# Products of ones in two idle stretches of TensorE, and other places for single blocks' outputs, row numbers and rows

## The chip, the cores and the metric

One core of a Trainium2 chip runs the whole program as one launch. The metric is the device time of one execution in microseconds (us); the median of several executions counts.

## The reference, cut to what matters

Two layers work on x of 16 × 256 tokens with 128 features, all in float32:

```
xn = layernorm(x)
s  = attention_0(xn)           # 16 heads of 64, two null keys, l2-normed q and k, ALiBi, causal
g  = silu(experts_0(xn))       # top-1 of 8 experts: gelu(x W1[e] + b1[e]) W2[e] + b2[e]
x  = x + s * g
xn = layernorm(x)
s  = attention_1(xn)           # one head of 128, causal, then layernorm and Wfc
g  = silu(experts_1(xn))       # top-2 of 8 experts, the two outputs weighted by their gates
x  = x + s * g
```

W1[e] is 128 × 512 and W2[e] is 512 × 128.

## The kernel before

**Order of the stages.** The program begins with norms and projections (0 to 59 us in the profile), then does attention steps b = 0 to 5 of layer 0 (to 319 us). Next come the experts of layer 0 (319 to 407 us), steps 6 to 15 with the first parts of layer 1 woven in, attention of layer 1, the experts of layer 1 (877 to 1026 us), and the combination of the two expert outputs. Each engine has its instructions in an order written out by hand; they meet through counting semaphores.

**Before the first scores.** TensorE does `tokens(0)` (transposes, L1233), then a list `RING_FIRST` of jobs that share two PSUM banks in turn: twelve `unit`s (a 128×512 projection each, L1285), then `("qk", i, 0)` (four transposes of a normed q or k part, L1304) in turn with the units of batch 1. Ahead of the first `qk` stands `nulls()` (L1451 to L1456). A `qk` waits until GpSimd has scaled its part (L1086), which comes behind a chain of Newton steps on GpSimd (L1081), which comes behind sums of squares on VectorE (L1873). From the unit `("unit", 2, 1)` on, `tokens(g)` and `logits(g)` (L1241, matmuls with 8 moving columns) are put between; `tokens(g)` waits for four tiles of `second_norm` on VectorE (L407).

**The expert stages.** Tokens are sorted by expert into rows in DRAM. A stage works through blocks j = 0, 1, 2, ...: double blocks of 256 rows (15 in layer 0, 31 in layer 1) and then 9 single blocks of 128 rows (j = 15 to 23 and 31 to 39). Block j uses buffer q = j % 4 for its weights, input rows, outputs `yb[:, q]` and row numbers `idx[:, q]`. For a block the engines do this:

- SyncE, step j: wait for `ye_evac` of block j, load weights (L688, 514 KB) and bias (L689) of block j + 4; wait for `xT_evac` of block j + 2, load the rows of block j + 6 (L683). All are issues of one queue, each behind a value that is read from a table.
- TensorE, step j: `turn(j+2)` (transpose the rows, L764), `up(j+1)` (L772), `down(j)` (L783).
- ScalarE: `gelu(j+1)` (L818); in layer 0 also `half_tanh` (L828).
- VectorE, step j: in layer 0 `silu2(j-1)` (L877); then `evac_x(j+2)` (row numbers L859, turned rows L860), then `add_b2(j)` (L868 for a double, L866 for a single block).
- GpSimd: `send(j)`, an indirect DMA for each 128 rows of output (L738), which adds 16 to `sent{q}` when it has landed.

`evac_x(j)` overwrites the row numbers of buffer q, so it waits until all earlier sends from that buffer have landed:

```
v.wait_ge(S["xT_full"], j + (base + 1))
if layer or not isinstance(j, int) or j >= NBUF:
    v.wait_ge(S[f"sent{q}"], sends(layer, j, q, i))
```

With `evac_x(j+2)` ahead of `add_b2(j)` in VectorE's order, a late send of block j - 2 holds up both.

Of the kernel before, what the change touches and what calls it, by code (L numbers as in the profile page):

```python
# [17 lines left out]
NB, N, D = 16, 256, 128  # L18
# [21 lines left out]
PERIOD = ((4, 11), (4, 27))  # L40
assert all((u - NSMALL) % 2 == 0 for u in UNITS_OF) and (NBLK0, NBLK1) == (24, 40)
# [73 lines left out]
def block_kernel(nc, a):  # L115
# [9 lines left out]
    with ctx:  # L125
# [130 lines left out]
        warm = take(1)  # L256
        LAST = (0, 1, 3, 2, 4, 6, 5, 7)
# [22 lines left out]
        def part(n):  # L280
# [6 lines left out]
        TAB = (TAB0, [FX, UX, CGX, HALF, UNI, FIRST, STEPS, CMP, RSJ])  # L287
        th = RA[:, SIZES[5] + SIZES[6]:SIZES[5] + SIZES[6] + 4 * D].rearrange("p (i n) -> p i n", i=2)
# [377 lines left out]

        def sends(layer, j, q, i):

            before = layer * sum(16 if m in SMALL[0] else 32 for m in range(q, NBLK0, NBUF))
            if isinstance(j, int):  # L670
                return before + sum(16 if m in SMALL[layer] else 32 for m in range(q, j, NBUF))
            n = 16 if q in SMALL_OF_FOUR[layer] else 32
            return i * n + (before + 32 - n)

        def ffn_sync(sp, layer, nblk, base, scattered, first_rows=None):
# [8 lines left out]

            def load_weights(j, q, i):
# [45 lines left out]
        def ffn_send(pool, layer, nblk, base):  # L731
            yb, idx = FFNB[layer][5:7]
# [12 lines left out]
            quads(pool, first, last, send)  # L745
            for j in range(last + 1, nblk):
                send(j, j % NBUF, j // NBUF)

        def all_sent(eng, layer):

            for q in range(NBUF):
                eng.wait_ge(S[f"sent{q}"], sends(layer, (NBLK0, NBLK1)[layer], q, 0))
# [4 lines left out]
        def ffn_tensor(pe, layer, nblk, base, counts, between=None):  # L757
# [3 lines left out]
            def turn(j, q, i):  # L761
                pe.wait_ge(S[f"rows_in{q}"], (i + (counts[q] + 1)) * 16)
                for t in range(1 if single(layer, j, q) else 2):
                    mm = pe.transpose(XT[q % 2][:, t * P:(t + 1) * P], xb[:, q, t, 0:D], ident)  # L764
# [43 lines left out]
        def ffn_scalar(act, layer, nblk, base, counts):  # L808
            HB = HBANKS[layer]
            wb, hT, yb = FFNB[layer][0], FFNB[layer][3], FFNB[layer][5]  # L810
# [11 lines left out]
            def half_tanh(j, q, first=False):  # L822
# [5 lines left out]
                act.activation(th[:, q % 2, 0:n], yb[:, q, 0:n], ACT.Tanh, scale=0.5).then_inc(S["tanh_done"], 1)  # L828
# [21 lines left out]
        def ffn_vector(v, layer, nblk, base, counts, flat=2 * NBUF, behind=None, between=None):  # L850
            XT, YB = bank[0:2], bank[6:8]
            _, b2b, xb, _, xbT, yb, idx = FFNB[layer]

            def evac_x(j, q, i):
                v.wait_ge(S["xT_full"], j + (base + 1))
                if layer or not isinstance(j, int) or j >= NBUF:
                    v.wait_ge(S[f"sent{q}"], sends(layer, j, q, i))
                n = 1 if single(layer, j, q) else 2
                v.tensor_copy(idx[:, q, 0:n], xb[:, q, 0:n, D].bitcast(I32))  # L859
                v.tensor_copy(xbT[:, q % 2, 0:n * BLK], XT[q % 2][:, 0:n * BLK]).then_inc(S["xT_evac"], 1)  # L860

            def add_b2(j, q, i):
                v.wait_ge(S["ye_full"], j + (base + 1))
                v.wait_ge(S[f"w_in{q}"], (i + (counts[q] + 1)) * 32)
                if single(layer, j, q):
                    ins = v.tensor_tensor(yb[:, q, 0:D], YB[q % 2][:, 0:D], b2b[:, q], ALU.add)  # L866
                else:
                    ins = v.tensor_tensor(yb[:, q, :].rearrange("p (t d) -> p t d", t=2),  # L868
# [4 lines left out]
            def silu2(j, q):  # L873
# [3 lines left out]
                v.scalar_tensor_tensor(out=yb[:, q, 0:n], in0=th[:, q % 2, 0:n], scalar=1.0, in1=yb[:, q, 0:n], op0=ALU.add,  # L877
# [349 lines left out]
        def _(pe):  # L1227
# [46 lines left out]

            pe.wait_ge(S["const_in"], 16)
# [196 lines left out]
            for use in RING_FIRST:  # L1472
# [875 lines left out]
```

## Time and profile before

| what | us |
|---|---|
| median of 3 runs (1060.01, 1060.05, 1069.24) | 1060.05 |
| the profiled execution | 1055.93 |
| its span, first to last instruction | 1054.1 |
| its mean granted TensorE clock | 0.981 |

The span and every start time are of the one profiled execution; the 1.8 us around it are start and end of the program. In the page, TensorE's matmuls are busy for 92% of the span, VectorE for 66%, GpSimd for 62%, ScalarE for 60%.

### The profile page before, as it was taken

The page shows a single profiled execution, that of the slowest core. Times are in us where ns is not written, and L with a number is a line of the kernel's source. Part 1 is how long each engine was busy: PE and PEld are TensorE (multiplying, and loading weights), DVE is VectorE, ACT ScalarE, POOL GpSimd, SP SyncE. Part 2 cuts the span into 40 slices and gives each one's busy share as a digit, 9 for nine tenths or more (in the row PEclk, how much of TensorE's full clock was granted, in tenths as well). Part 3 has the DMA queues.
Part 4 walks back from the last instruction along what each step waited for, and adds up shares of the span by engine and source line. Part 5 has one row for each costly group of instructions (what it writes and reads, how often), then busy time and mean ns, then how long its engine had stood idle before and what let it go on. Part 6 is the DMA issues. An engine that isn't in the chain of part 4 may idle for free.

```text
span 1054.1 us, 21432 instructions
## 1 busy us (share of the span) xinstructions
PE 965.7 (92%) x6330; PEld 695.2 (66%) x6330; DVE 691.8 (66%) x2589; ACT 631.3 (60%) x1945; POOL 650.7 (62%) x803
## 2 busy tenths in 40 slices
PE   5788799999998978999999999999898899999965
PEld 2565466666668976666665665556666788999955
DVE  6977777886773324867778677677885574445634
ACT  4348767767765546677776775766665564444432
POOL 4663588788756543676686668788746651555540
PEclk9789999999999999999999999999999999999997
DMA  9400202302337764033031230321222035787758
GB/s 292 78 7 1 47 27 62 73 26 60 84 104 181 216 204 117 6 75 65 16 70 25 46 70 26 70 56 50 55 66 68 31 102 136 227 231 226 214 168 240
DMA packets 95444, 103.20 MB, mean 98 GB/s; under 512 B 10095, under 2 KB 83030, under 8 KB 95088
## 3 DMA queue, kind: packets, MB, share of 16 engines
q1 hardware_dynamic: 88752, 89.36, 33.4%
q0 software_dynamic: 6592, 12.65, 3.5%
q8 instruction: 45, 0.74, 0.3%
q14 instruction: 55, 0.45, 0.1%
HBM read 77.54 MB, written 23.50 MB: 96 GB/s over the span
## 4 chain that ended last, share of the span: by engine, by line
PE 54%; DVE 18%; ACT 8%; POOL 7%; issue 6%; DMA 5%; SPq 1%; POOLq 0%; DVEq 0%; ACTq 0%
PE bank L1285 10%; PE bank L772 7%; PE bank L1314 7%; PE bank L783 7%; PE bank L1341 5%; DVE arena L1973 5%; ACT arena L1697 4%; PE bank L1329 4%; PE bank L1304 4%; PE bank L1364 3%; DMA expert_out<-RA 2%; DVE arena L1982 2%; DMA expert_out<-arena 2%; POOL arena L1071 2%; DVE arena L1873 2%
## 5 line engine op out<-in xcount | busy, mean ns | idle before, releaser
L1697 ACT ACTIVATE arena<-arena 128x128 f32<-128x128 f32 (+1 forms) x512 | 226.9, 446 | 102.1 <-DVE arena L1973 101.8
L1973 DVE CUSTOM_DVE_ANT_0 arena<-bank,arena 128x128 f32<-128x128 f32 (+1 forms) x512 | 183.1, 413 | 115.2 <-PE bank L1314 112.3
L1285 PE MATMUL bank<-arena 128*128 128x512 f32 x384 | 211.4, 637 | 7.7 <-ACT arena L1686 5.2
L1071 POOL TENSOR_TENSOR arena<-arena 128x512 f32<-128x512 f32 x128 | 133.3, 1045 | 127.8 <-ACT arena L1673 108.7
L1982 DVE COPY arena<-bank 128x384 f32<-128x384 f32 x256 | 130.1, 549 | 21.3 <-PE bank L1329 21.0
L1086 POOL TENSOR_TENSOR arena<-arena 128x512 f32<-128x512 f32 x128 | 129.8, 1050 | 1.3
L1673 ACT ACTIVATE arena<-bank 128x512 f32<-128x512 f32 x192 | 112.7, 587 | 27.7 <-PE bank L1285 27.4
L1329 PEld LDWEIGHTS bank<-const,arena 128*128 128x128 f32 x768 | 91.4, 142 | 55.6 <-issue 55.2
L738 POOL DMA_INDIRECT expert_out<-arena x71 | 71.3, 1005 | 90.8 <-DVE arena L868 40.5
L1314 PE MATMUL bank<-arena 64*128 64x128 f32 (+1 forms) x1024 | 118.5, 350 | 6.6 <-DVE arena L1973 6.0
L1341 PE MATMUL bank<-arena 128*64 128x256 f32 (+1 forms) x1024 | 112.2, 340 | 6.6 <-DVE arena L1982 6.2
L818 ACT ACTIVATE arena<-bank,arena 128x256 f32<-128x256 f32 (+1 forms) x160 | 59.0, 451 | 85.1 <-PE bank L772 85.1
L1314 PEld LDWEIGHTS bank<-arena 64*128 64x128 f32 x1024 | 67.0, 186 | 65.0 <-issue 50.2
L1341 PEld LDWEIGHTS bank<-arena 128*64 128x64 f32 x1024 | 62.4, 136 | 68.9 <-issue 34.6
L638 POOL DMA_INDIRECT expert_rows<-XN,slots x92 | 91.8, 998 | 25.7 <-issue 19.4
L1329 PE MATMUL bank<-const,arena 128*128 128x128 f32 x768 | 106.1, 275 | 0.0
L1697 ACT ACTIVATION_READ_ACCUMULATOR arena<-arena 128x1 f32 x512 | 97.6, 191 | 0.0
L1873 DVE TENSOR_REDUCE arena<-arena 128x8 f32<-128x512 f32 x128 | 84.3, 679 | 13.4 <-POOL arena L1071 13.0
L1304 PE MATMUL bank<-const,arena 128*128 128x128 f32 x512 | 81.7, 289 | 11.0 <-POOL arena L1086 7.3
L1110 POOL TENSOR_TENSOR arena<-arena 128x512 f32<-128x512 f32 x64 | 79.6, 1276 | 14.8 <-DMA arena<-recip_rows 14.8
L1081 POOL TENSOR_TENSOR arena<-arena 128x64 f32<-128x64 f32 x192 | 60.8, 316 | 40.3 <-DVE arena L1886 26.1
L1285 PEld LDWEIGHTS bank<-arena 128*128 128x128 f32 x384 | 60.6, 194 | 33.5 <-issue 23.3
(302 smaller groups left out, 1641.3 us busy)
## 6 DMA issues: line engine op xcount, KB each, us to landing
arena<-in_wp SPq DMA_DIRECT2D x40, 514.0 KB
arena<-recip_rows SPq DMA_DIRECT2D x30, 512.0 KB, 6.4
XN<-in_wp SPq DMA_DIRECT2D x24, 514.0 KB
arena<-expert_rows SPq DMA_DIRECT2D x46, 129.0 KB
arena<-in_b SPq DMA_DIRECT2D x64, 64.0 KB
arena<-expert_out SPq DMA_DIRECT2D x16, 256.0 KB, 5.2
expert_out<-fill SPq DMA_DIRECT2D x11, 338.6 KB
expert_rows<-fill SPq DMA_DIRECT2D x1, 2644.5 KB, 21.7
```

Source lines behind the costliest of these rows:

```text
L1071: pool.tensor_tensor(sq[:, i % 2], r, r, ALU.mult).then_inc(S["sq_done"], 1)
L1086: pool.tensor_tensor(raw[:, t, 512 * k:512 * k + 512].rearrange("p (h d) -> p h d", d=DH), raw[:, t, 512 * k:512 * k + 512].rearrange("p ( ...
L1285: mm = pe.matmul(RING[bnk][:, :], xa[:, p, t * P:(t + 1) * P], wqkv[:, 512 * k:512 * k + 512], start=True, stop=True)
L1304: mm = pe.transpose(RING[bnk][:, P * c:P * c + P], raw[:, t, 512 * k + P * c:512 * k + P * c + P], ident)
L1314: mm = pe.matmul(SBANK[k][:, P * t:P * t + n], qT[r:r + 64, p, c, t * P:(t + 1) * P], kT[r:r + 64, p, c, 0:n], start=True, stop=True)
L1329: mm = pe.transpose(TBANK[k][:, P * j:P * j + P], SPb[:, c % 2, 384 * k + P * j:384 * k + P * j + P], ident)
L1341: mm = pe.matmul(OB[64 * k:64 * k + 64, N * (c % 2) + P * j:N * (c % 2) + N], Vt[:, p, j, DH * h:DH * h + DH], PTb[:, c % 2, 384 * k + N * ...
L1673: ins = act.activation(dst, src[:, :], ACT.Copy)
L1697: ins = act.activation(w, w, ACT.Exp, bias=nm[:, p, 16 * t + h:16 * t + h + 1], scale=-1.0, accum_out=den[:, p, 16 * t + h:16 * t + h + 1])
L1873: v.tensor_reduce(ss[:, t, 8 * k:8 * k + 8], sq[:, i % 2].rearrange("p (h d) -> p h d", d=DH), AX.X, ALU.add).then_inc(S["ss_done"], 1)
L1973: ins = v.tensor_tensor_reduce(out=SPb[:, c % 2, 384 * k + P * t:384 * k + P * t + n], in0=SBANK[k][:, P * t:P * t + n], in1=alibi[:, h, N ...
L1982: v.tensor_copy(PTb[:, c % 2, 384 * k:384 * k + 384], TBANK[k][:, 0:384]).then_inc(S["pt_evac"], 1)
```

## The change

**Products of ones.** TensorE multiplies the 128×128 tile `ones` with itself into a PSUM bank that nothing reads yet, 10 times at its start (behind `ones_ready`, ahead of the constants' wait and `tokens(0)`) and 20 times between `nulls()` and the first `qk`.

**Places.** A block's outputs and row numbers now have a place k = `PLACES[layer][j]`; places 0 to 3 are the old buffers, others are new memory (`OWN`). In layer 0 the single blocks j = 15 to 23 get places 4, 5, 6, 3, 0, 1, 2, 4, 5. The places from 4 on share one semaphore, `sent4`; `evac_x` waits on it once, at j = 22, for the sends of blocks 15, 16 and 17. `evac_x(18)` to `evac_x(21)` wait for the sends of blocks 11 to 14. In layer 1 each single block has a place of its own and `evac_x` waits for no send. Double blocks keep their buffers and waits.

**Rows of layer 1's single blocks.** They no longer go through the four row buffers. SyncE loads them into a tile `SROWS` with nine places: five of the loads stand in steps 1, 5, 9, 13 and 17, four in steps 20 to 23, each behind the step's weights. TensorE waits for all nine before it turns the first. The nine row loads of steps 25 to 33, with their waits, are gone.

```diff
+PLACES = (tuple(j % 4 if j < 15 else (4, 5, 6, 3, 0, 1, 2, 4, 5)[j - 15] for j in range(NBIG[0] + NSMALL)),
+          tuple(j % 4 if j < NBIG[1] else 4 + j - NBIG[1] for j in range(NBIG[1] + NSMALL)))
+AGAIN = (22, None)
@@ ffn_sync, step
                 load_weights(j + NBUF, q, i + 1)
-                if more:
+                if layer and q == 1 and not isinstance(j, int):
+                    load_single(i)
+                if layer and isinstance(j, int) and last <= j < last + NSMALL - last // NBUF:
+                    load_single(j - last + last // NBUF)
+                if more and not (layer and single(1, j + NBUF + 2 if isinstance(j, int) else j, q)):
                     sp.wait_ge(S["xT_evac"], j + (base + 3))
                     load_rows(j + NBUF + 2, (q + 2) % NBUF, i + (q + 2 + NBUF) // NBUF)
@@ ffn_send
-                        yt[layer][:, :], bass.IndirectOffsetOnAxis(ap=idx[:, q, t:t + 1], axis=0), yb[:, q, t * D:(t + 1) * D], None,
-                        bounds_check=(1 + layer) * T - 1, oob_is_err=False).then_inc(S[f"sent{q}"], 16)
+                        yt[layer][:, :], bass.IndirectOffsetOnAxis(ap=numbers(layer, j, q)[:, t:t + 1], axis=0),
+                        outputs(layer, j, q)[:, t * D:(t + 1) * D], None,
+                        bounds_check=(1 + layer) * T - 1, oob_is_err=False).then_inc(S[sender(layer, j, q)], 16)
@@ ffn_tensor, turn
+                if layer and single(1, j, q):
+                    pe.wait_ge(S["single_rows"], NSMALL * 16)
+                    mm = pe.transpose(XT[q % 2][:, 0:P], SROWS[:, j - NBIG[1], 0:D], ident)
@@ ffn_vector, evac_x
-                if layer or not isinstance(j, int) or j >= NBUF:
-                    v.wait_ge(S[f"sent{q}"], sends(layer, j, q, i))
+                if place(layer, j, q) < NBUF and (layer or not isinstance(j, int) or j >= NBUF):
+                    v.wait_ge(S[sender(layer, j, q)], sends(layer, j, q, i))
+                if j == AGAIN[layer]:
+                    v.wait_ge(S[f"sent{NBUF}"], sent_by(layer, NBUF, j))
@@ tensor
+            def keep_running(n, out):
+                for _ in range(n):
+                    pe.matmul(out[:, 0:P], ones[:, :], ones[:, :], start=True, stop=True)
+            pe.wait_ge(S["ones_ready"], 1)
+            keep_running(10, TBANK[1])
             pe.wait_ge(S["const_in"], 16)
             tokens(0)
...
                 if use == ("qk", 0, 0):
                     nulls()
+                    keep_running(20, TBANK[1])
```

## Rows read from the trace of the kernel before

**Rows 1.** The page, part 4: the chain that ended last, by engine.
```profile
PE 54%; DVE 18%; ACT 8%; POOL 7%; issue 6%; DMA 5%; SPq 1%; POOLq 0%; DVEq 0%; ACTq 0%
```

**Rows 2.** That chain in order of time: start, length, what.
```profile
9.40 4.54 DMA small<-in_L_attn_k_scale
...
33.98 1.05 POOL arena L1086
```

**Rows 3.** Timeline of TensorE, 0 to 75 us: start, length, work, [idle before].
```profile
9.21 1.09 PE L1233 MATMUL bank<-const,arena 128*128 128x128 f32 x4 [9.21 <-DVE arena L407]
...
35.17 2.09 PE L1304 MATMUL bank<-const,arena 128*128 128x128 f32 x8 [7.30 <-POOL arena L1086]
37.09 2.08 PE L1285 MATMUL bank<-arena 128*128 128x512 f32 x2
...
45.38 0.60 PE L1233 MATMUL bank<-const,arena 128*128 128x128 f32 x4
...
46.26 1.10 PE L1285 MATMUL bank<-arena 128*128 128x512 f32 x2
```

**Rows 4.** Busy by stretch: engines in order, then granted clock, DMA share, GB/s.
```profile
30.00:32.00 2.00, 0.00 (x0) 0.00 (x0) 1.86 (x21) 0.00 (x0) 1.63 (x5) 0.80 1.04 192
...
44.00:46.00 2.00, 2.00 (x9) 1.26 (x9) 2.00 (x6) 1.01 (x2) 1.04 (x1) 0.78 0.00 0
...
64.00:66.00 2.00, 1.77 (x12) 1.26 (x13) 0.81 (x7) 1.73 (x8) 1.61 (x6) 0.84 0.26 78
```

**Rows 5.** Timeline of VectorE, 42 to 52 us.
```profile
42.03 1.08 DVE L407 TENSOR_SCALAR arena<-RS_,small,arena 128x128 f32<-128x128 f32 x1
...
43.73 2.96 DVE L407 TENSOR_SCALAR arena<-RS_,small,arena 128x128 f32<-128x128 f32 x8
...
51.39 0.25 DVE L1936 TENSOR_SCALAR arena<-bank,small 128x32 f32<-128x32 f32 x1 [1.73 <-PE bank L1462]
```

**Rows 6.** Waits of layer 0's singles, 370 to 410 us: total, times, longest.
```profile
DVE RA L859 <- DMA expert_out<-RA: 16.5, 9, 4.5
```

**Rows 7.** The same for layer 1's singles, 985 to 1030 us.
```profile
DVE arena L859 <- DMA expert_out<-arena: 13.9, 10, 2.5
```

**Rows 8.** Timeline of TensorE, layer 0's single blocks: up(16), up(17), up(23).
```profile
380.19 1.16 PE L772 MATMUL bank<-RS_,XN 128*128 128x128 f32 x8 [1.94 <-DVE RS_ L860]
...
382.19 1.12 PE L772 MATMUL bank<-RS_,XN 128*128 128x128 f32 x8
...
402.66 1.16 PE L772 MATMUL bank<-RS_,XN 128*128 128x128 f32 x8 [1.27 <-DVE RS_ L860]
```

**Rows 9.** Timeline of VectorE: add_b2(15).
```profile
382.28 0.29 DVE L866 TENSOR_TENSOR RA<-bank,arena 128x128 f32<-128x128 f32 x1 [0.18 <-PE bank L783]
```

**Rows 10.** Timeline of SyncE's queue, layer 0: rows (L683) and weights (L688).
```profile
378.19 0.50 SPq L683 DMA_DIRECT2D arena<-expert_rows  x1
...
383.94 0.34 SPq L688 DMA_DIRECT2D XN<-in_wp  x1
...
389.06 0.34 SPq L688 DMA_DIRECT2D XN<-in_wp  x1
...
390.68 0.34 SPq L683 DMA_DIRECT2D arena<-expert_rows  x1
391.79 0.34 SPq L688 DMA_DIRECT2D XN<-in_wp  x1
```

**Rows 11.** Busy by stretch, behind the load issued at 383.94.
```profile
388.00:388.50 0.50, 0.33 (x3) 0.33 (x3) 0.32 (x2) 0.15 (x1) 0.00 (x0) 1.00 0.38 107
```

**Rows 12.** Timeline of SyncE's queue, layer 1: weights of block 34.
```profile
1001.21 0.34 SPq L688 DMA_DIRECT2D arena<-in_wp  x1
```

**Rows 13.** Timeline of TensorE, layer 1: up(39).
```profile
1021.24 1.16 PE L772 MATMUL bank<-arena 128*128 128x128 f32 x8 [1.02 <-DVE arena L860]
```

**Rows 14.** DMA queues, layer 1's singles (1001 to 1018 us): packets, MB, share.
```profile
q1 hardware_dynamic: 2369, 3.56, 77.3%
q0 software_dynamic: 256, 0.39, 6.2%
```

More of the change, by code:

```diff
@@ L256, in block_kernel @@
         warm = take(1)
+        SROWS = take(NSMALL * ROW).rearrange("p (k d) -> p k d", k=NSMALL)
+        YROWS1 = take(NOWN[1] * ROW).rearrange("p (k d) -> p k d", d=ROW)
         LAST = (0, 1, 3, 2, 4, 6, 5, 7)
@@ L665, in entry, with place, outputs, numbers @@
             return i * (NBUF - len(few)) + (len(few) + q - k)
+        def place(layer, j, q):
+            return PLACES[layer][j] if isinstance(j, int) else q
+        def outputs(layer, j, q):
+            k = place(layer, j, q)
+            n = 1 if single(layer, j, q) else 2
+            return OWN[layer][:, k - NBUF, 0:D] if k >= NBUF else FFNB[layer][5][:, k, 0:n * D]
+        def numbers(layer, j, q):
+            k = place(layer, j, q)
+            n = 1 if single(layer, j, q) else 2
+            return OWN[layer][:, k - NBUF, D:D + 1].bitcast(I32) if k >= NBUF else FFNB[layer][6][:, k, 0:n]
+        def sent_by(layer, k, last):
+            return sum(16 if m in SMALL[layer] else 32 for m in range(last) if min(PLACES[layer][m], NBUF) == k)
+        def sender(layer, j, q):
+            return f"sent{min(place(layer, j, q), NBUF)}"
         def sends(layer, j, q, i):
-            before = layer * sum(16 if m in SMALL[0] else 32 for m in range(q, NBLK0, NBUF))
+            k = place(layer, j, q)
+            before = layer * sent_by(0, k, NBLK0)
             if isinstance(j, int):
-                return before + sum(16 if m in SMALL[layer] else 32 for m in range(q, j, NBUF))
-            n = 16 if q in SMALL_OF_FOUR[layer] else 32
-            return i * n + (before + 32 - n)
+                return before + sent_by(layer, k, j)
+            return i * 32 + before
         def ffn_sync(sp, layer, nblk, base, scattered, first_rows=None):
@@ L749, in all_sent @@
         def all_sent(eng, layer):
-            for q in range(NBUF):
-                eng.wait_ge(S[f"sent{q}"], sends(layer, (NBLK0, NBLK1)[layer], q, 0))
+            for k in range(NPLACES):
+                eng.wait_ge(S[f"sent{k}"], layer * sent_by(0, k, NBLK0) + sent_by(layer, k, (NBLK0, NBLK1)[layer]))
         HBANKS = (bank[2:6], bank[4:6] + bank[2:4])
@@ L761, in turn @@
             def turn(j, q, i):
-                pe.wait_ge(S[f"rows_in{q}"], (i + (counts[q] + 1)) * 16)
-                for t in range(1 if single(layer, j, q) else 2):
-                    mm = pe.transpose(XT[q % 2][:, t * P:(t + 1) * P], xb[:, q, t, 0:D], ident)
+                if layer and single(1, j, q):
+                    pe.wait_ge(S["single_rows"], NSMALL * 16)
+                    mm = pe.transpose(XT[q % 2][:, 0:P], SROWS[:, j - NBIG[1], 0:D], ident)
+                else:
+                    pe.wait_ge(S[f"rows_in{q}"], (i + (counts[q] + 1)) * 16)
+                    for t in range(1 if single(layer, j, q) else 2):
+                        mm = pe.transpose(XT[q % 2][:, t * P:(t + 1) * P], xb[:, q, t, 0:D], ident)
                 mm.then_inc(S["xT_full"], 1)
@@ L809, in ffn_scalar @@
             HB = HBANKS[layer]
-            wb, hT, yb = FFNB[layer][0], FFNB[layer][3], FFNB[layer][5]
+            wb, hT = FFNB[layer][0], FFNB[layer][3]
             def gelu(j, q, i):
@@ L827, in half_tanh @@
                 n = D if single(layer, j, q) else 2 * D
[L828 removed]
+                act.activation(th[:, q % 2, 0:n], outputs(layer, j, q), ACT.Tanh, scale=0.5).then_inc(S["tanh_done"], 1)
             def both(j, q, i):
@@ L851, in ffn_vector @@
             XT, YB = bank[0:2], bank[6:8]
-            _, b2b, xb, _, xbT, yb, idx = FFNB[layer]
+            _, b2b, xb, _, xbT, _, _ = FFNB[layer]
             def evac_x(j, q, i):
                 v.wait_ge(S["xT_full"], j + (base + 1))
-                if layer or not isinstance(j, int) or j >= NBUF:
-                    v.wait_ge(S[f"sent{q}"], sends(layer, j, q, i))
+                if place(layer, j, q) < NBUF and (layer or not isinstance(j, int) or j >= NBUF):
+                    v.wait_ge(S[sender(layer, j, q)], sends(layer, j, q, i))
+                if j == AGAIN[layer]:
+                    v.wait_ge(S[f"sent{NBUF}"], sent_by(layer, NBUF, j))
                 n = 1 if single(layer, j, q) else 2
-                v.tensor_copy(idx[:, q, 0:n], xb[:, q, 0:n, D].bitcast(I32))
+                ids = SROWS[:, j - NBIG[1]:j - NBIG[1] + 1, D] if layer and n == 1 else xb[:, q, 0:n, D]
+                v.tensor_copy(numbers(layer, j, q), ids.bitcast(I32))
                 v.tensor_copy(xbT[:, q % 2, 0:n * BLK], XT[q % 2][:, 0:n * BLK]).then_inc(S["xT_evac"], 1)
```

19 lines of the change are left out of this document (13 added, 6 removed).

## Prediction

> **What bounds the kernel now.** I read the chain of work that ended last first, by engine and then in order of time. TensorE holds 54% of it and VectorE 18% [rows 1]; no single engine is the bound, so each edit has to be priced where it stands. In order of time the chain leaves TensorE alone up to 35 us: it goes from a small load that lands at 13.94 through sums on VectorE to the Newton steps on GpSimd and the first scaled part at 33.98 [rows 2]. From 35.17 it is TensorE, which had stood idle for 7.30 us [rows 3]. Its granted clock fell in that gap and was back only near 45 us [rows 4]: at 37.09 a unit (x2) takes 2.08 us, at 46.26 the same takes 1.10 us [rows 3].
>
> In the expert stages I read the waits and then the timelines. In both layers' single blocks VectorE's longest waits are at L859, for a send to land: nine of them, 16.5 us, in layer 0 [rows 6] and ten, 13.9 us, in layer 1 [rows 7]. TensorE passes them on: up(16) and up(23) come behind waits of 1.94 and 1.27 us, while up(17), which found its rows, came 2.00 us behind up(16) [rows 8]. From up(17) to up(23) are 20.47 us, 3.41 for each block against 2.00 without waits.
>
> **Ten products at the start.** A float32 product has two records (a unit is x2). Four records took 1.09 us at 9.21 against 0.60 at 45.38 [rows 3], so the clock there is the lower of 1.2 and 2.4 GHz, although no fall is recorded. Twenty records at 0.27 us are 5.4 us, inside the 9.21 us in which TensorE is idle. They delay nothing. If they raised the clock in time, the first units would be faster, but up to 33.98 the chain is a load, VectorE and GpSimd [rows 2]. Price 0; on either side I leave 0.3 us.
>
> **Twenty products before the first qk.** Forty records of 128 columns at full clock cost about 0.125 us each (eight in 1.16 less the tail, [rows 8]): 5.0 us, from 27.87 to 32.9. The first qk can't start before GpSimd's part at 35.1 [rows 2], so they delay nothing, and 2.3 us of idle time are left where there were 7.30. Before, the fall came between 30 and 32 (a mean of 0.80, [rows 4]), over 2 us behind the last work. I take it that the clock stays up.
>
> What is the gain? At full clock the sequence from the second qk on, which GpSimd releases at 36.1, is: qk 0.5, unit 0.9, logits 0.8, then (qk 0.45, unit 0.9) twice, up to 41 us, where it stood at 45.38. Then `tokens(1)` waits for VectorE: four tiles end at 42.03 + 1.08 = 43.11 [rows 5]. That is the new limit: 45.38 − 43.11 = 2.27 us earlier. `tokens(2)` needs four of the eight tiles from 43.73 at 0.37 each, 45.2 us; it stood some 2.0 us later. VectorE itself waited 1.73 us at 51.39 [rows 5] and hardly elsewhere before the first scores, so it can follow by little more than that. **I take 1.9 us.** From below, 0 (the clock falls all the same and stays down as long); from above 3.4, with 1.5 us for the units behind 65 us that now run in a second cold stretch [rows 4].
>
> A rule speaks against this: the Trainium skill ("TensorE: Matmul & The Clock Gate", Part 1) says that the monitor's looks run free of the kernel's start. By it the rest of the gap can meet one of them wholly in one run and not in another. In 64 to 66 the clock fell although matmuls are recorded for 1.77 of 2 us [rows 4]. I weigh this as a rival; its cost is softened, since 2.1 us (41 to 43.11) of the new sequence is slack before VectorE.
>
> **Layer 0's single blocks.** All sends' waits go for blocks 15 to 17; for 18 to 21 they look at blocks 11 to 14, which are sent seven steps before; at 22, VectorE waits for block 17, five steps back. Behind these waits stand `evac_x` and `add_b2` on VectorE, and with them TensorE and SyncE. What is late next? Three things:
> - TensorE: 2.00 us a block [rows 8].
> - The loop of the weights. up(16) began at 380.19 and add_b2(15) ended at 382.28 + 0.29 = 382.57 [rows 9], 2.38 us later. SyncE then needs 0.77 us before a weights' load starts (a rows' issue ended at 390.68 + 0.34 = 391.02, the weights' behind it began at 391.79, [rows 10]). The load issued at 383.94 [rows 10], with bias and rows behind it, had all but left the engines in 388 to 388.5 [rows 11], 4.3 us after its issue; I take 4.2. The loop is 2.38 + 0.77 + 4.2 = 7.35 us for three blocks, 2.45 for each.
> - SyncE's queue: weights at 389.06 and again at 391.79, 2.73 us, of which the rows cost 391.79 − 390.68 = 1.11 [rows 10]. In layer 0 they stay in steps up to 17.
>
> The 16 DMA engines as a whole: in layer 1's singles 3.56 MB took 77.3% of 17 us, 271 GB/s, and 0.39 MB of sends 6.2% [rows 14]. Weights and bias (592 kB) are 2.18 us, rows 0.24, a send 0.18: 2.60 us in layer 0.
>
> So SyncE's 2.73 us is the limit. The rows' issue at 378.19 + 0.50 is now followed by the weights of 18 at 379.46, of 19 at 382.2, 20 at 384.9, 21 at 387.7, 22 at 390.4, and of 23, without rows before it, at 392.0. up(23) can start 4.2 us later at 396.2, or 2.00 us behind up(22) (394.6), at 396.6. It stood at 402.66 [rows 8]: **6.0 us**. Bounds: 1.8, if loads need 6.0 us (the loop is then 3.05 us and begins 1.8 us later), 6.6 if they need 3.6.
>
> **Layer 1's single blocks.** No waits for sends, and nine rows' loads fewer, so SyncE's step is 1.62 us and no bound. Two remain: the loop, 2.45, and the engines, 2.18 + 0.18 = 2.36 us. The weights of block 34 were issued at 1001.21 [rows 12], which is not changed, and land at 1005.4. Five blocks on, up(39) is at 1005.4 + 5 × 2.45 = 1017.65 by the loop and 1017.2 by the engines; it stood at 1021.24 [rows 13]. **3.8 us**; bounds 0 and 5.5.
>
> The other side of this is nine more issues in the double blocks' steps. A step there is 2.73 us of SyncE's work [rows 10], 3.84 with the extra rows, in a block's time of 3.8 us (some 32.5 blocks from the stage's start at 877 to 1001.21, [rows 12]). In four steps running it may be over by 0.1, 0.5 us in all, and weights are asked for nearly three blocks, 11 us, ahead. All nine have landed over 10 us before `turn(31)`. Price 0 to 0.5. Copies, products and sends of a block are as many as before; only their addresses change.
>
> **Sum.** 1.9 + 6.0 + 3.8 = 11.7 us on the profiled execution's 1055.93: 1044.2. The median of the runs is 4.1 us above it (1060.05), which I carry: **1048.3 us**. The stages behind each gain are chained to its end, so I let it pass through in full.
>
> **Rivals.**
> - *The loads are next, and slower than now.* With the sends' pauses gone, the engines' load rises from some 84% (77.3 + 6.2, [rows 14]) to near 97%, and a load may need 5.2 us. The loop is then 2.8 us: layer 0 loses 1.0 us by its first load and little more, layer 1 saves 1021.24 − (1006.4 + 14.0) = 0.8. With 1.9: 1.9 + 4.9 + 0.8 = 7.6, **1052.4**. For it: the engines are near full. Against it: the load of rows 10 and 11 was met by others and took 4.3. The Trainium skill ("DMA: Bandwidth & Descriptors", Latency and other measured facts) gives HBM an average 0.2 us and 2 us at high load; by it a load would be up to 1.8 us longer, which no run here shows.
> - *The clock falls before the scores all the same.* Only the singles gain: 9.8, **1050.2**.
> - *The clock gains more.* A cold stretch behind 65 us goes too: 13.2 to 14, **1046.5**.
> - *Slower.* Unpaced, sends and loads pile up: each load behind one or two others. From 5.6 us a load on, layer 1's loop (3.15 + 5.6)/3 = 2.9 is as slow as its blocks are now; layer 0's at 7.1. At 9.5 us the loops are 4.2: layer 1 loses 6 × 1.3, layer 0 6 × 0.8 = 12.6 in all, less 1.9: **1070.8**. Against it: loads share 16 engines, and the sum of work a block, 2.36 to 2.60 us, is below every period before.
> - *It doesn't do what it says*, a wait for sends staying at block 22: block 17's sends must land within three steps, 8 us, against some 5. At most 1 us.
>
> **How the numbers follow.** The forecast, 1048.3, has 0.55 and spans 1046.8 to 1050 by the bounds of the loads (3.6 to 4.8 us). Loads next: 0.2. Clock falls: 0.1. Clock gains more: 0.11. Slower: 0.04. Eight in ten reach from 1045 to 1053.5, with the loads' rival inside. About 1% (10.6 us) is what a measurement of this kernel tells from no change. Faster by more than that means under 1049.45: 0.5 of the forecast's 0.55, the clock's 0.11 and a little of the rivals, 0.64; slower by over 1% 0.03; the rest, 0.33, lies between, nearly all of it on the fast side.
>
> **What would show it.** Granted clock 1.00 in 30 to 44 us; the unit behind qk(1) near 1.1 us; `tokens(1)` about 43.1 and behind VectorE. In both layers' singles no wait of L859 for a send, up to up 2.4 to 2.8 us, SyncE's weights 2.73 us apart in layer 0. A wait of L772 or L764 for a weights' load of over a microsecond is right; loads over 5 us from issue are the first rival. I am wrong if the first scores don't come 1.5 us earlier, or up(39) lies less than 2 us nearer to up(31).

## The result and the profile after

| | before | after |
|---|---|---|
| median, us (12 runs each) | 1060.84 | 1054.96 (1051.31 to 1060.77) |
| ratio | | 0.9932 [0.9909, 0.9956] |
| profiled execution, us | 1055.93 | 1053.28 |
| its span, mean granted clock | 1054.1, 0.981 | 1051.5, 0.984 |

The ratio is that of the mean times: 7.2 us of 1060 (4.7 to 9.6), within 1% and on the fast side. The medians lie 5.9 us apart. Forecast were 11.7 us; 1054.96 lies 1.5 us above the end of the range.

**The start.** The page's chain by engine, to be set beside [rows 1], and TensorE's timeline from 0 to 46 us (start, length, work, [idle before]):

```profile
PE 51%; DVE 17%; ACT 8%; issue 7%; POOL 7%; DMA 5%; SPq 4%; POOLq 0%; DVEq 0%; ACTq 0%
```

```profile
1.37 4.64 PE L1328 MATMUL bank<-ones 128*128 128x128 f32 x20 [1.37 <-POOL ones L1109]
9.28 1.09 PE L1283 MATMUL bank<-const,arena 128*128 128x128 f32 x4 [3.27 <-DVE arena L419]
...
27.69 4.63 PE L1328 MATMUL bank<-ones 128*128 128x128 f32 x40
35.10 2.09 PE L1361 MATMUL bank<-const,arena 128*128 128x128 f32 x8 [2.78 <-POOL arena L1136]
37.03 2.08 PE L1342 MATMUL bank<-arena 128*128 128x512 f32 x2
...
45.34 0.60 PE L1283 MATMUL bank<-const,arena 128*128 128x128 f32 x4
```

SyncE's queue and DMA have 9% of this chain where they had 6%, but 6% again in a second profile of the same kernel (e15 below), so the shares show no new limit. The ones run where they should, and the idle time before the first `qk` is 2.78 instead of 7.30 us. But the unit behind it still takes 2.08 us and `tokens(1)` stands at 45.34 (45.38 before, [rows 3]). The busy times by stretch (engines in order, then granted clock, DMA share, GB/s) say why:

```profile
32.00:34.00 2.00, 0.32 (x3) 0.13 (x2) 1.83 (x6) 0.00 (x0) 1.61 (x6) 1.00 1.04 194
34.00:36.00 2.00, 0.90 (x4) 0.72 (x4) 1.97 (x2) 0.00 (x0) 2.00 (x3) 0.65 0.92 187
36.00:44.00 8.00, 8.00 (x26) 5.25 (x25) 7.83 (x15) 3.17 (x5) 6.98 (x8) 0.50 0.03 6
44.00:46.00 2.00, 2.00 (x10) 1.25 (x10) 2.00 (x6) 1.05 (x2) 1.22 (x1) 0.79 0.00 0
```

The clock fell 3.4 us later than before [rows 4], still ahead of the `qk`, and came back at the same 44.9.

**Layer 0's single blocks.** The waits from 370 to 410 us (engine, line, what for: total, times, longest) hold none of L909 for a send; [rows 6] had 16.5 us of them. This stands in their place:

```profile
PE bank L818 <- DMA arena<-in_b: 4.4, 5, 1.7
```

SyncE's queue: the weights of blocks 20, 21, 22 and 23; and TensorE: up(20) and up(23).

```profile
386.37 0.34 SPq L727 DMA_DIRECT2D XN<-in_wp  x1
...
389.14 0.34 SPq L727 DMA_DIRECT2D XN<-in_wp  x1
...
391.90 0.34 SPq L727 DMA_DIRECT2D XN<-in_wp  x1
...
395.49 0.34 SPq L727 DMA_DIRECT2D XN<-in_wp  x1
```

```profile
392.39 1.13 PE L818 MATMUL bank<-RS_,XN 128*128 128x128 f32 x8 [1.72 <-DMA arena<-in_b]
...
399.46 1.13 PE L818 MATMUL bank<-RS_,XN 128*128 128x128 f32 x8 [0.22 <-DMA arena<-in_b]
```

SyncE's step is 2.77 us, as forecast (2.73). But the load issued at 386.37 let up(20) start only at 392.39, 6.0 us later, and the next in that loop (the weights of block 23) left at 395.49, another 3.10 us on (forecast 2.38 + 0.77 = 3.15). So this turn of the loop was 9.12 us for three blocks, 3.04 each, against the 2.45 forecast: the one wrong number is the load's 4.2 us. The next load in it took 3.97 us; for the blocks 17 to 23 the time from issue to up has a mean of 5.0. up(23) came at 399.46, 3.20 us earlier than in [rows 8]; the stage itself is 4.56 us shorter, but up(15) had come 1.36 us later.

**Layer 1's single blocks.** TensorE's up(33), up(34) and up(39), and what VectorE did between the first two:

```profile
1002.18 1.13 PE L818 MATMUL bank<-arena 128*128 128x128 f32 x8 [0.57 <-DMA arena<-in_b]
1006.01 1.13 PE L818 MATMUL bank<-arena 128*128 128x128 f32 x8 [1.70 <-DVE arena L910]
...
1018.64 1.13 PE L818 MATMUL bank<-arena 128*128 128x128 f32 x8 [0.60 <-DMA arena<-in_b]
```

```profile
1004.24 0.29 DVE L916 TENSOR_TENSOR arena<-bank,arena 128x128 f32<-128x128 f32 x1 [0.95 <-PE bank L829]
1004.45 1.28 DVE L2246 TENSOR_TENSOR arena<-const,small 128x512 f32<-128x512 f32 x2
1005.65 0.15 DVE L909 COPY arena<-arena 128x1 int32<-128x1 int32 x1
1005.71 0.28 DVE L910 COPY arena<-bank 128x128 f32<-128x128 f32 x1
```

up(39) came 2.60 us earlier than in [rows 13]. Besides the loads there is a wait that I hadn't named: `evac_x(34)` stands behind a pair of products for the diagonal tiles (L2246, 1.28 us), which the sends' waits had hidden. up(31) to up(39) is 2.20 us shorter; 2 us was the prediction's own least.

### The profile page after: what moved, and what is told of

It is laid out like the page before. It is cut to its first block, busy times and chain, and to the rows that moved or that the text cites. A ratio compares the mean times of both kernels' runs of the same rounds, so it can differ in the third digit from the quotient of the medians.

```text
span 1051.5 us, 21545 instructions
## 1 busy us (share of the span) xinstructions
PE 972.7 (93%) x6390; PEld 702.2 (67%) x6390; DVE 692.4 (66%) x2589; ACT 631.4 (60%) x1945; POOL 651.1 (62%) x803
## 4 chain that ended last, share of the span: by engine, by line
PE 51%; DVE 17%; ACT 8%; issue 7%; POOL 7%; DMA 5%; SPq 4%; POOLq 0%; DVEq 0%; ACTq 0%
PE bank L1342 10%; PE bank L818 7%; PE bank L829 7%; PE bank L1371 6%; PE bank L1398 5%; DVE arena L2031 4%; ACT arena L1755 4%; PE bank L1386 4%; PE bank L1361 4%; PE bank L1421 3%; DVE arena L2040 2%; DVE arena L1931 2%; POOL arena L1121 2%; DMA arena<-in_b 2%; POOL arena L1160 1%
## 5 line engine op out<-in xcount | busy, mean ns | idle before, releaser
L1136 POOL TENSOR_TENSOR arena<-arena 128x512 f32<-128x512 f32 x128 | 129.8, 1051 | 1.3
L1371 PE MATMUL bank<-arena 64*128 64x128 f32 (+1 forms) x1024 | 118.5, 350 | 6.4 <-DVE arena L2031 5.8
L1371 PEld LDWEIGHTS bank<-arena 64*128 64x128 f32 x1024 | 67.0, 186 | 64.8 <-issue 50.2
L1398 PEld LDWEIGHTS bank<-arena 128*64 128x64 f32 x1024 | 62.4, 136 | 68.9 <-issue 34.6
L650 POOL DMA_INDIRECT expert_rows<-XN,slots x92 | 92.1, 1001 | 25.7 <-issue 19.3
L1131 POOL TENSOR_TENSOR arena<-arena 128x64 f32<-128x64 f32 x192 | 60.8, 317 | 40.3 <-DVE arena L1944 26.1
```

The source lines that it names most:

```text
L1136: pool.tensor_tensor(raw[:, t, 512 * k:512 * k + 512].rearrange("p (h d) -> p h d", d=DH), raw[:, t, 512 * k:512 * k + 512].rearrange("p ( ...
L1371: mm = pe.matmul(SBANK[k][:, P * t:P * t + n], qT[r:r + 64, p, c, t * P:(t + 1) * P], kT[r:r + 64, p, c, 0:n], start=True, stop=True)
L1398: mm = pe.matmul(OB[64 * k:64 * k + 64, N * (c % 2) + P * j:N * (c % 2) + N], Vt[:, p, j, DH * h:DH * h + DH], PTb[:, c % 2, 384 * k + N * ...
```

## The experiments

Each ratio of mean times is to the kernel before on the same chip. The chips differ: the median of before was 1062.4 us on the first and the fourth group's, 1087.4 and 1083.5 us on the second's and third's. I also read each trace in stages; all in us. "first" is the start of the second group of scores (L1371 after, L1314 before), "cold" the stretch with the lower clock around the first `qk`, "up 0" the start of layer 0's first up; then up(15) to up(23) of layer 0, up(0) to up(31) and up(31) to up(39) of layer 1.

| kernel | ratio, 95% | first | cold | up 0 | 15–23 | 0–31 | 31–39 |
|---|---|---|---|---|---|---|---|
| before | | 64.56 | 31.2–44.9 | 319.25 | 27.37 | 117.85 | 24.08 |
| after | 0.9932 [.9909, .9956] | 64.52 | 34.6–44.9 | 319.47 | 22.81 | 119.29 | 21.88 |
| e1 | 1.0001 [.9975, 1.0026] | 64.57 | 34.6–44.8 | 321.86 | 26.24 | 118.18 | 26.22 |
| e2 | 0.9908 [.9888, .9928] | 64.27 | 31.0–44.6 | 319.20 | 24.19 | 118.95 | 21.51 |
| e3 | 0.9922 [.9889, .9955] | 62.62 | none | 318.90 | 24.46 | 118.60 | 21.93 |
| e4 | 0.9891 [.9869, .9914] | 62.34 | 35.5–38.9 | 323.14 | 21.84 | 119.09 | 19.16 |
| e5 | 1.0104 [1.0060, 1.0148] | 63.17 | 36.5–39.9 | 320.31 | 29.68 | 128.52 | 24.74 |
| e6 | 0.9970 [.9945, .9994] | 72.62 | 47.6–54.4, 57.8–78.3 | 327.37 | 24.83 | 122.92 | 24.33 |
| e7 | 0.9957 [.9929, .9984] | 64.30 | 36.8–40.2 | 320.42 | 22.25 | 121.84 | 23.24 |
| e8 | 0.9917 [.9890, .9943] | 62.67 | none | 319.39 | 24.33 | 123.38 | 26.06 |
| e9 | 0.9975 [.9949, 1.0002] | 64.72 | 34.4–44.6 | 325.26 | 22.80 | 122.08 | 28.09 |
| e10 | 0.9978 [.9947, 1.0009] | 62.94 | 32.1–38.9 | 319.44 | 29.16 | 122.08 | 22.32 |
| e11 | 0.9934 [.9905, .9963] | 64.19 | 34.1–44.3 | 323.08 | 24.22 | 121.99 | 22.18 |
| e12 | 0.9913 [.9877, .9949] | 63.95 | 33.8–44.0 | 324.18 | 24.04 | 121.61 | 21.84 |
| e13 | 0.9927 [.9901, .9953] | 62.43 | 31.2–38.0 | 317.92 | 22.75 | 118.32 | 21.08 |
| e14 | 0.9923 [.9892, .9955] | 65.25 | none | 321.85 | 22.11 | 119.06 | 20.94 |
| e15 | 0.9924 [.9898, .9950] | 63.49 | 37.0–43.8 | 318.15 | 22.79 | 119.19 | 21.50 |
| e16 | 0.9881 [.9837, .9924] | 65.16 | 31.9–45.5 | 319.83 | 21.84 | 118.21 | 20.91 |

**e1, the ones alone** (before with both calls of `keep_running`).

> The kernel before with the 10 and 20 products of ones alone. Theory A (the products end 2.8 us ahead of the first qk, and the clock falls all the same): tokens(1) at 45.3 to 45.4 us as in both kernels, time within 1 us of before. Rival B (the phase of the clock's fall was bad luck in the one profile shown): clock at full speed from 28 to 64 us here, tokens(1) near 43.1, 2 us off the time.

Nothing, to a quarter of a per cent, 2.7 us on either side; `tokens(1)` came at 45.39.

**e2, the places alone** (after without the calls).

```diff
-            pe.wait_ge(S["ones_ready"], 1)
-            keep_running(10, TBANK[1])
...
-                    keep_running(20, TBANK[1])
```

> The changed kernel without any product of ones. Theory A (all of the gain is in the single blocks): the same time as the changed kernel, 5 to 7 us under before, and both stages of single blocks as in the changed kernel's profile (22.8 us from up(15) to up(23), 19.1 us from up(32) to up(39)). Rival B (the products matter in runs whose profile is not shown): 1 to 2 us slower than the changed kernel.

0.9908, at least all of the gain. The ones add nothing to it that these intervals could show.

**e3, 33 products** instead of 20, so that they reach the `qk`.

> The changed kernel with 33 products ahead of the first qk in place of 20, which fills the gap up to about 35.0 us. Theory A (the clock needs the work to reach the first qk): no fall at 34.7 us, the second qk and the first unit of batch 1 at full clock, tokens(1) at 43.1 to 43.5 behind VectorE, 1.9 us off the time against the changed kernel. Rival B (transposes and logits of 8 columns don't hold the clock): it falls at 38 or 41 us and tokens(1) comes at 43.5 to 45. Rival C (products of ones don't count as activity at all): fall at 34.7 as before, no gain.

Here the clock held up to 62.2. `tokens(1)` came at 42.02 (forecast 43.1) and `tokens(2)` waits for VectorE; the scores are 1.94 us earlier than before, the forecast's 1.9. The ratio (0.9922) is within the interval of the change's. TensorE in e3, ones to units behind the scores, and the busy times of two stretches:

```profile
27.83 7.53 PE L1328 MATMUL bank<-ones 128*128 128x128 f32 x66
...
42.02 0.66 PE L1283 MATMUL bank<-const,arena 128*128 128x128 f32 x4 [0.30 <-DVE arena L419]
...
45.21 0.66 PE L1283 MATMUL bank<-const,arena 128*128 128x128 f32 x4 [1.23 <-DVE arena L419]
...
60.42 1.98 PE L1291 MATMUL bank<-small,RA 128*128 128x8 f32 x16
62.62 1.65 PE L1371 MATMUL bank<-arena 64*128 64x128 f32 x8 [0.22 <-DVE arena L2031]
64.20 2.07 PE L1342 MATMUL bank<-arena 128*128 128x512 f32 x2
```

```profile
60.00:62.00 2.00, 2.00 (x19) 1.95 (x20) 1.89 (x10) 0.68 (x2) 0.65 (x3) 1.00 0.00 0
62.00:69.00 7.00, 6.78 (x22) 3.58 (x21) 4.96 (x18) 4.24 (x17) 6.22 (x13) 0.52 0.06 20
```

But the clock fell as the matmuls with 8 moving columns ended, with TensorE busy, for 6.9 us where it was 3.4 before, and by layer 0's first up 0.35 us are left.

**e8, a second gap too** (no ones at the start, 33 before the `qk`, 12 in step 0).

```diff
                     turn_p(b, c)
+                    if isinstance(b, int) and b == 0 and c == 1:
+                        keep_running(12, MISC)
```

> The changed kernel without the 10 products at the start, with 33 ahead of the first qk and 12 more in TensorE's idle stretch of the first attention step, 72.6 to 75.6 us. Theory A (what the 33 gain is given back in later cold stretches): first scores at 62.6, clock up or back by 69, the unit at 74 to 75 us at full clock, and layer 0's first up at 317.5 to 318, 1 to 2 us under e3's 318.9. Rival B (the chain behind 65 us is VectorE's and the clock there costs nothing): layer 0's first up as in e3.

With the 12 products the clock stayed up from 66.2 to 107.1. Against after, its TensorE is 1.9 to 2.1 us ahead at 57.8 and still at 107. Then the clock falls at 107.1, where after's stayed up, and 0.5 to 0.9 us are left at 111. At 113 VectorE's 8 elements of L533 take 1.01 us while GpSimd is in L1136, and at 124 the two kernels are level. VectorE's L533 in after, the same and GpSimd's work beside it in e8, and TensorE in e8:

```profile
114.24 0.16 DVE L533 TENSOR_SCALAR arena<-arena 128x8 f32<-128x8 f32 x1
```

```profile
113.29 1.01 DVE L533 TENSOR_SCALAR arena<-arena 128x8 f32<-128x8 f32 x1
```

```profile
112.18 2.10 POOL L1136 TENSOR_TENSOR arena<-arena 128x512 f32<-128x512 f32 x2
```

```profile
124.15 1.10 PE L1340 MATMUL bank<-arena 128*128 128x512 f32 x2 [1.77 <-ACT arena L1744]
```

This is no accident of one run. In the 18 profiles of this document the operation took 0.16 us in ten, where a 128×64 operation of GpSimd ended 0.03 us into it, and 1.01 to 1.06 us in eight (e1, e4, e5, e8, e9, e11, e12, e14), where a 128×512 operation of GpSimd had just begun; there it ended 0.03 us behind that one.

**e4, a quarter of the weights** (single blocks load 256 of 1028 columns and leave out the rest).

> The changed kernel, but a single block's weights are loaded only in their first 256 of 1028 columns, 128 KB in place of 514 KB; the other columns keep what an earlier block left. Theory A (weights' loads are the next limit in the single blocks): up to up falls to 2.0 to 2.8 us in both layers (SyncE's 2.8 us in layer 0, TensorE's 2.0 in layer 1), so up(15) to up(23) in some 20 us for 22.8 and up(32) to up(39) in some 15 us for 19.1, in all 5 to 7 us off the changed kernel. Rival B (SyncE's queue is the limit in both): layer 0 as in the changed kernel, layer 1 2 us less at most. Rival C (the bias, which is the last to land, is slow in itself): no change in either.

Against after, layer 1 gained 2.7 us and layer 0 1.0; the ratio is 4.4 us under after's, where 5 to 7 were expected. With 128 KB of weights instead of 514, and the 64 KB of bias as before, TensorE's blocks that waited for a load in layer 0 came 3.6 to 4.5 us behind its issue (3.9 to 6.2 in after), with SyncE's steps at 2.8 to 3.0. So a third of the bytes kept some four fifths of the time (a mean of 3.9 against 4.9 us). How much of that is the bias, which is issued 0.5 us later and lands last, e4 doesn't tell. The Trainium skill ("DMA: Bandwidth & Descriptors", Anatomy of one DMA) states, for transfers that GpSimd issues, a fixed 2.0 us in each, most of it the receipt of the last write. By its fit, taken for SyncE's loads with weights and bias as one transfer, they would be 2.5 and 3.4 us alone: an estimate, which lies below what both took here beside others.

**e5, the bias ahead of the weights.**

```diff
+                sp.dma_start(b2b[:, q], ...)
                 sp.dma_start(wb[:, q], ...)
-                sp.dma_start(b2b[:, q], ...)
```

> The changed kernel with a block's bias load issued ahead of its weights' load instead of behind it. Theory A (the bytes of a load in a full queue are the limit, and the bias only marks their end): last landing is the weights', single blocks within 0.5 us of the changed kernel in both layers, same time. Rival B (the bias' own 3.3 us from issue to landing, begun 0.5 us behind the weights, is what TensorE waits for): up to up shorter by up to 0.3 us a block, 2 to 4 us in both layers.

A clear loss: 1.0% against the kernel before. Since the edit is to the change, the order alone costs more, 1.7 to 1.8% against the change's ratio (0.9932 and 0.9924, on other chips) and 1.9% against e8's on this chip. TensorE's waits from 375 to 415 us in e5 and in e12, which has the old order:

```profile
PE bank L818 <- DMA XN<-in_wp: 8.7, 4, 4.5
```

```profile
PE bank L818 <- DMA arena<-in_b: 5.8, 7, 1.4
```

Against e6 to e8 on the same chip, layer 0's double blocks (62.64 against 57.6 to 59.6) lost 3 to 5 us and layer 1's 5 to 7 as well. There sends landed later too: from 900 to 990 us VectorE waited 28.9 us for them, 18.3 in e6. Why the other order costs so much isn't settled.

**e6, layer 1's rows through the old buffers**, with the outputs in their own places.

> The changed kernel with layer 1's single rows through the four row buffers, as before; outputs and row numbers keep their own places. Theory A (the early rows cost about 1 us in the double blocks and spare SyncE and the engines in the single ones): up(0) to up(31) in layer 1 back from 118.6 to 119.3 us to about 118.0; up(32) to up(39) 20 to 20.5 us against 18.7 to 19.1; the total within 1 us of the changed kernel. Rival B (SyncE's 2.8 us a step is the limit of these blocks): up(32) to up(39) 20.5 to 21.3, slower by 1 to 2 us. Rival C (the early rows cost nothing): up(31) as in the changed kernel.

up(31) to up(39) took 24.33, which lies between e7's 23.24 and e8's 26.06 with early rows on the same chip. The stage doesn't tell them apart. The ratio is 0.5% above e8's, with intervals that just don't meet, but e8 has other products of ones and the plain change wasn't run on that chip: undecided.

**e7, layer 0's rows early** (those of blocks 18 to 23 loaded in steps 4 to 9 into `RA`, over tokens of later attention steps, which are lost).

> The changed kernel, and in layer 0 the rows of blocks 18 to 23 loaded into places of their own in steps 4 to 9, as layer 1 has it. Theory A (SyncE's queue, 2.8 us a step, and full loads both hold layer 0's single blocks): up(15) to up(23) from 22.8 to 24.5 down to 20.5 to 22, 1 to 2.5 us off the time, with up to 1 us given back in double blocks. Rival B (only the bytes count, they are as many): up(15) to up(23) within 0.7 us of the changed kernel.

22.25 in the singles, above the 20.5 to 22 of the expectation, but up(0) to up(15) took 59.63 where e6 and e8 have 58.35 and 57.55: given back.

**e9 and e10, one layer's places each; e12, both (e2 again)**, without ones.

```diff
-          tuple(j % 4 if j < NBIG[1] else 4 + j - NBIG[1] for j in range(NBIG[1] + NSMALL)))
+          tuple(j % 4 for j in range(NBIG[1] + NSMALL)))
```

> The change without products of ones and with layer 1 as before (its outputs, row numbers and rows in the four buffers); only layer 0's single blocks have places of their own. Theory (each layer's places give what its single blocks save, and it passes through): 3 to 4.5 us faster than before, up(15) to up(23) 22.8 to 24.5 us (27.4 before), up(32) to up(39) 21 to 23.4 as before. Rival 1 (the gain of layer 0 is given back in steps 6 to 15): within 1.5 us of before. Rival 2 (nearly all of the gain is layer 0's): 7 us or more faster. The double blocks of layer 1, with no early row loads, should take what before's take; if they are as long as those of the full change, the early row loads don't lengthen them.

> The change without products of ones and with layer 0 as before; layer 1's single blocks have places of their own and early rows. Theory: 2 to 3 us faster than before, up(32) to up(39) 18.7 to 19.1 us (21.3 before), up(15) to up(23) of layer 0 27 as before, and about 1 us of it given back in layer 1's double blocks (up(0) to up(31) 118.6 to 119.3 against 117.9) if the early row loads cost that. Rival (the early row loads cost nothing, the double blocks differ by chance): double blocks within 0.5 us of e9_layer0_only's and 3 to 5 us faster in all.

> The change without products of ones once more (the same kernel as e2_places_only), beside its two halves on one chip. If the halves add up, its gain is the sum of those of e9_layer0_only and e10_layer1_only within 2 us, and 8 to 12 us as in the first measurement. If the gains are not additive (one layer's gain is lost when the other's is there, or a common part is counted twice), it is off by more than 3 us.

Each stage moved in its half and not in the other: 22.80 against 29.16, and 22.32 against 28.09. The double blocks are equal (122.08 twice, 121.61), one profile each, so nine early row loads cost them nothing that shows; the 1.4 us by which after's profile is longer there than before's is not theirs. The ratios gave 0.25%, 0.22% and together 0.87%; the sum is 4.3 us short, outside my 2 us and beyond the 3 us that I had set for gains that don't add, with an uncertainty of about 6. Neither half alone is clear of no change. Whether something passes through only when both are there stays open.

**e11, the products for the diagonals two pairs a step in blocks 28 to 30.**

> The change without products of ones, and VectorE's six pairs of products for the diagonal tiles (1.3 us each) done two pairs a step behind add_b2 of blocks 28 to 30 instead of one pair a step behind 28 to 33. Theory (up(34) comes 3.6 to 3.8 us behind up(33) because evac_x(34) stands behind such a pair and add_b2): up(33) to up(34) 2.0 to 2.8 us and up(32) to up(39) 17.2 to 18 us instead of 18.7; in exchange the double blocks 29 to 31 may take up to 1 us more. Time 0 to 1.5 us below e12_places_again. Rival (the weights' loads hold block 34, and VectorE is merely late beside them): up(34) waits for in_b instead, nothing is saved. Slower rival: the double blocks lose more than 1.5 us, as VectorE is nearly full there.

up(33) to up(34) fell to 2.12 us, from 3.13 in e12 on the same chip (2.7 to 3.95 in the others with layer 1's new places). But up(33) now waits 0.83 us for VectorE, four later blocks wait 0.7 to 1.0 us each for their loads, and up(31) to up(39) stayed at 22.18. A wait that stood beside the loads' loop, not in it.

**e13, the bias on a semaphore of its own; e14, the same with e8's ones; e15, the full change again; e16, no bias loads in single blocks** (which then add another block's bias).

```diff
-                pe.wait_ge(S[f"w_in{q}"], (i + (counts[q] + 1)) * 32)
+                pe.wait_ge(S[f"w_in{q}"], (i + (counts[q] + 1)) * 16)
```

> The change without products of ones; the bias counts on a semaphore of its own, so up and gelu wait for the 514 KB of weights alone and only add_b2 waits for the bias, which is issued 0.5 us behind them. Theory (it is the bias, landing last, that holds TensorE in the single blocks): TensorE's waits for in_b go, layer 0's up(15) to up(23) falls from 24 to 21.5 to 23 us and layer 1's up(32) to up(39) from 19 to 17.5 to 18.5; 1 to 3.5 us below e15_change_again and e2_places_only's 0.991. Rival (the weights land just as late, the bias was only the last name in one semaphore): TensorE waits for in_wp as long as it did for in_b, no gain beyond 1 us.

> e13_bias_apart with the products of ones of e8_clock_two_gaps (33 ahead of the first qk, 12 in step 0). Theory (what the clock gains ahead of the scores is lost by 124 us to a later cold stretch and to VectorE): within 1 us of e13_bias_apart, layer 0's up(0) within 1 us of its. Rival (the clock is worth something in the median though not in a profile): 1.5 us or more below e13_bias_apart.

> The full change once more, beside the others on one chip. Theory (what was measured is the sum of some 3.5 us in each layer's single blocks and nothing else): 0.991 to 0.995 of before, up(15) to up(23) 22.5 to 24.5, up(31) to up(39) 21.5 to 23. The forecast's 11.7 us would be 0.989.

> The change without products of ones; single blocks load no bias (the buffer keeps that of the double block before, so the outputs of the single blocks have another expert's bias). SyncE's step in layer 0 loses one issue of three. Theory (SyncE's issues and the last landing are layer 0's limit): weights of layer 0's singles 2.2 to 2.4 us apart instead of 2.8, up(15) to up(23) 20.5 to 22.5 us; layer 1, where SyncE's step is only two issues, gains less, 0.5 to 1.5 us. Rival (the 514 KB of weights are the limit): up(15) to up(23) within 0.7 us of e13_bias_apart's. Slower is not expected.

In e13 the wait took the other name and stayed. Its waits and DMA issues (KB each, median us to landing) in layer 0, 375 to 405 and 378 to 394 us:

```profile
PE bank L819 <- DMA XN<-in_wp: 3.9, 5, 2.0
```

```profile
XN<-in_wp SPq DMA_DIRECT2D x6, 514.0 KB, 4.6
...
arena<-expert_rows SPq DMA_DIRECT2D x5, 64.5 KB, 3.6
```

The trace tells the landing of one load of the six: 4.6 us behind its issue, and of one in layer 1 (1000 to 1014 us): 5.0. The blocks that waited for weights in layer 0 came 3.9 to 5.1 us behind the issue, a mean of 4.5. Both stages are 0.4 to 1.4 us shorter than e2's and e12's, but not shorter than e15's in layer 0, nor is the ratio lower (0.9927 against e15's 0.9924). e16 removes one of SyncE's three issues, and its weights are still 2.66 us apart (377.66 to 390.97, five steps), since they wait for blocks that wait for loads. The stage, 21.84 us, is 0.9 shorter than e13's. With SyncE's step out of the way the landing is the limit; in after both are, since its weights of blocks 18 to 22 are 2.8 to 2.9 us apart. e14 is within 1 us of e13 in time, as expected, but its up 0 is 3.9 us later, and its first scores come at 65.25. Its 33 products began at 29.39, 1.6 us later than e3's, and held up the first `qk` until 36.76, though GpSimd's part was there at 35.44; then the clock fell at 55.0. Neither e13, e14 nor e16 beats e2 by more than the intervals.

## Why the prediction was wrong

The forecast's 11.7 us miss what the stages gave by 4.3: 1.9 in the clock's term, 2.2 in layer 0's and 0.2 in layer 1's.

**Products at the start: right.** Free, and without an effect that shows (e1).

**"I take it that the clock stays up": the step that failed, 1.9 us.** Twenty products end 2.78 us ahead of the `qk`, and the clock fell there; the first scores came 0.04 us earlier where less than 1.5 was to show me wrong. My own rival held. But the step was wrong in a second way. e3 and e8 have the 1.9 us at the scores, as I had worked it out, and by layer 0's first up it is gone: up 0 lies between 318 and 327 us whatever the ones do (327 in e6, whose clock stayed low from 57.8 to 78.3). Nor is it the products' alone: e13 and e10, with no ones at all, have a short cold stretch by themselves (31.2 to 38.0, 32.1 to 38.9) and their first scores at 62.43 and 62.94, while e14, with 33 products, has them at 65.25. "The stages behind each gain are chained to its end, so I let it pass through in full" is false for the attention steps. There are seven profiles of kernels with the same 20 products. In six (after, e1, e4, e5, e7, e15) the clock fell between 34.6 and 37.0 and was up again anywhere from 38.9 to 44.9. In the seventh, e6, it held through the first `qk` to 47.6, as I had taken it to, with `tokens(1)` at 42.18:

```profile
28.86 4.63 PE L1320 MATMUL bank<-ones 128*128 128x128 f32 x40
35.18 0.63 PE L1353 MATMUL bank<-const,arena 128*128 128x128 f32 x4 [1.69 <-POOL arena L1128]
```

The 33 products held it through the `qk` in all three (e3, e8, e14); with none it fell between 31.0 and 34.4 in all eight. The Trainium skill ("TensorE: Matmul & The Clock Gate", Part 1) says that the monitor's looks run free of the kernel's start; these profiles agree, and a rule that I priced at 0.1 should have kept me from taking one profile's cold stretch as the kernel's.

**Layer 0, 6.0 us: the mechanism right, the size off.** No wait for sends is left, SyncE's step is 2.77 us, the rest of the loop 3.10. The failed term is "I take 4.2" for a load. It was read from one load in a stretch with pauses; at full pace the blocks that waited came 3.9 to 6.2 us behind the issue in after (a mean of 4.9) and 4.5 to 5.7 in e2 (5.1), for the weights alone 4.5 (e13). By my own formula, 8 blocks × (5.0 − 4.2) / 3 = 2.1 us. The stage should have come to 27.37 − 6.0 = 21.4; the nine profiles with layer 0's new places and unchanged loads (after, e2, e3, e6, e8, e9, e11, e12, e15) have a mean of 23.8. The three with the old (before, e1, e10) have 27.6: a gain of **3.8 us**. Each of these three has a stretch of low clock of 3.4 to 6.8 us in the stage (from 389.6, 389.5 and 390.5), none of the nine has; a part of the gain may be that, which I hadn't priced.

**Layer 1, 3.8 us: right in size, for a wrong reason in part.** The stage was to fall from 24.08 to 20.3. With the new places (after, e2, e3, e7, e8, e10, e12, e15) it has a mean of 22.5, 2.2 us longer, by the same loads. But 24.08 was a fast sample: before, e1 and e9 have a mean of 26.1. A gain of **3.6 us**. The means are of few profiles and mix chips: where before takes some 1061 us the two gains are 3.2 and 3.4 us, on the third group's chip 5.5 and 6.0, where the ratios of e9 and e10 kept 2.7 and 2.4.

**Early row loads, 0 to 0.5 us: right**, by e9 against e10 and e12.

**The sum.** 0 + 3.8 + 3.6 = 7.4 us, against 7.2 measured in the full change, 8.1 when repeated (e15), 9.8 and 9.4 without ones (e2, e12). The close match is in part luck, as the gains by chip show. The profiled spans differ by only 2.6 us: single blocks 6.8 shorter, but after's double blocks are 1.1 (layer 0) and 1.4 us longer and up(23) to layer 1's up(0), which the change doesn't touch, 1.4 (476.65 us in before, 478.00 in after, 475.52 in e15). That is variation between profiles.

**The rivals.** I held "the loads are next" (5.2 us a load) and "the clock falls" apart, as if one of them could happen. Both did: 4.9 + 0.8 without the clock is 5.7 us, 1054.3 by my own terms, beyond my range's 1053.5. That this meets the median so well is luck: its terms for the two layers, 4.9 and 0.8, were measured as 3.8 and 3.6. The slower rival was wrong: in after no block came more than 6.2 us behind a load that it waited for, far from 9.5. e5 shows that a loss was to be had by order alone.

## What to carry to other kernels

When a wait is removed from a loop that prefetches, price the transfer at the new pace, not from one in a stretch with pauses; a small step in its latency is divided by the depth of the loop but counts in every block. Let independent rivals happen together before setting the range. A stretch of low clock in one profile is a sample: look at two or three profiles of the same kernel before counting on it, and follow the gained time to the next place where another engine is late.

## What the runs showed of the hardware

- The clock fell with TensorE recorded as fully busy: at 62.2 in e3, as the last of 16 matmuls with 8 moving columns ran, and at 55.0 in e14, 0.2 us behind 16 with 4. The same 16 with 4 columns ran in e3 from 51.94 and the clock stayed up. The engines in e14 from 54 to 58 us:

```profile
54.00:55.00 1.00, 1.00 (x11) 1.00 (x11) 1.00 (x4) 0.00 (x0) 0.00 (x0) 0.98 0.00 0
55.00:58.00 3.00, 3.00 (x11) 1.86 (x9) 3.00 (x8) 1.19 (x2) 1.15 (x2) 0.50 0.00 0
```

- Work alone doesn't bring it back. In e6, which differs from after only in layer 1, it stayed low for 20 us of recorded matmuls, through the last small ones before the scores, and the second group of scores came 8 us late:

```profile
58.00:78.00 20.00, 20.00 (x77) 14.88 (x76) 9.39 (x33) 7.57 (x23) 11.40 (x20) 0.50 0.02 8
```

- Blocks that waited for a load of 128 KB plus 64 KB came 3.6 to 4.5 us behind its issue (e4), for one of 514 plus 64 KB 3.9 to 6.2 (after).
- An operation of VectorE on 128×8 elements took 0.16 us in ten profiles and 1.01 to 1.06 in eight. In the eight it began within 0.12 us of an operation of GpSimd that takes 1.05 to 1.10 us, and ended 0.03 us behind it. No run takes GpSimd's operation away by itself.
- Putting the 64 KB broadcast ahead of the 514 KB instead of behind made the kernel 1.0% slower than before [0.6, 1.5], where the change had made it 0.7% faster.
